# Attention rows: both images of a step taken together, and the middle channel tile ahead of the third

## What is computed

```
x = x + outlook(group_norm(x))    # 6 heads, softmax over 3x3 neighbours, weighted values, projection
x = x + window(group_norm(x))     # shifted 7x7 windows, 12 heads of 16 channels:
    qkv  = xw @ qkv_weight.T + qkv_bias
    attn = softmax(q * hd**-0.5 @ k.T + rel_pos_bias + mask)
    out  = (attn @ v) @ proj_weight.T + proj_bias
```

## Time and profile before

| what | value |
|---|---|
| median of three runs | 3687.9 us |
| the profiled execution | 3694.54 us, of which its span is 3692.7 us |
| mean granted TensorE clock | 0.949 of full speed |
| PE busy | 3321.1 us, 90% of the span |
| DVE, POOL, ACT busy | 74%, 65%, 51% |

### The profile page before, as it was taken

The page is one execution under the profiler, slowest core; times in us unless marked ns, Lnnn a source line. Parts: engine busy times, 40 slices in busy tenths (PEclk is TensorE's granted clock), DMA queues, the critical chain, the costliest instruction groups (busy, mean ns, idle before and its releaser), DMA issues.

```text
span 3692.7 us, 105251 instructions
## 1 busy us (share of the span) xinstructions
PE 3321.1 (90%) x39908; PEld 1964.0 (53%) x39908; DVE 2743.5 (74%) x4465; ACT 1869.8 (51%) x3602; POOL 2413.9 (65%) x1888
## 2 busy tenths in 40 slices
PE   5999989899899988988889888898989989899988
PEld 3456644566445664456643566346663466634665
DVE  4967779677796777967779677786767867687676
ACT  3445544555435554455543555435554455544555
POOL 2767747676476764767647676477765777566774
PEclk7999989999899998999989999999989999899998
DMA  4732237222371223712246222561215512165122
GB/s 105 141 80 67 73 77 138 65 82 62 84 142 49 83 75 76 143 52 75 76 87 131 64 71 67 105 128 56 83 50 115 121 52 84 55 126 110 56 74 60
DMA packets 204343, 317.51 MB, mean 86 GB/s; under 512 B 16922, under 2 KB 176154, under 8 KB 203802
## 3 DMA queue, kind: packets, MB, share of 16 engines
q0 software_dynamic: 31936, 148.66, 20.7%
q1 hardware_dynamic: 171866, 161.61, 15.0%
HBM read 45.97 MB, written 38.54 MB: 23 GB/s over the span
## 4 chain that ended last, share of the span: by engine, by line
PE 44%; POOL 16%; issue 16%; ACT 11%; DVE 8%; DMA 4%; DVEq 0%; POOLq 0%; SPq 0%; ACTq 0%
POOL sp__70 L1767 6%; POOL sp__70 L1774 4%; PE P L485 4%; DMA prod<-prod 4%; PE P L726 3%; PE P L649 3%; PE P L713 3%; DVE prod L1419 3%; POOL xr L1760 3%; PE P L647 3%; PE P L651 3%; ACT kbd L1095 2%; ACT kbd L1094 2%; DVE sp__70 L1523 2%; PE P L694 2%
## 5 line engine op out<-in xcount | busy, mean ns | idle before, releaser
L1774 POOL TENSOR_TENSOR sp__70<-sp__70,rc 128x588 f32<-128x588 f32 x512 | 600.9, 1174 | 465.1 <-DVE rc L1540 459.2
L1419 DVE TENSOR_TENSOR prod<-P,vpad 128x896 f32<-128x896 f32 (+1 forms) x768 | 791.3, 1051 | 140.1 <-PE P L485 126.7
L1537 DVE TENSOR_REDUCE sm<-sp__70 128x12 f32<-128x588 f32 x512 | 390.8, 763 | 479.7 <-ACT sp__70 L1112 479.6
L1767 POOL TENSOR_TENSOR sp__70<-sp__70,mx 128x588 f32<-128x588 f32 x512 | 598.0, 1173 | 217.8 <-DVE mx L1530 217.6
L1112 ACT ACTIVATE sp__70<-sp__70 128x588 f32<-128x588 f32 x512 | 358.2, 700 | 706.0 <-POOL sp__70 L1767 705.9
L485 PE MATMUL P<-at,sel 108*128 108x448 bf16 x1512 | 429.5, 363 | 63.1 <-DVE prod L1419 32.9
L1523 DVE TENSOR_TENSOR sp__70<-P,relb 128x588 f32<-128x588 f32 x512 | 389.6, 761 | 119.8 <-PE P L713 114.1
L1687 POOL DMA_DIRECT2D prod<-prod x216 | 202.5, 941 | 373.4 <-DVE prod L1419 369.9
L1530 DVE TENSOR_REDUCE mx<-sp__70 128x12 f32<-128x588 f32 x512 | 389.3, 760 | 9.1
L1120 ACT ACTIVATE pt<-P 98x588 f32<-98x588 f32 x512 | 311.7, 663 | 128.6 <-PE P L726 126.7
L726 PE MATMUL P<-ident,sp__70 113*98 113x113 f32 x3072 | 354.2, 267 | 19.5 <-DVE sp__70 L1523 19.5
(11 more groups left out here) (255 smaller groups left out, 7356.9 us busy)
## 6 DMA issues: line engine op xcount, KB each, us to landing
prod<-prod POOLq DMA_DIRECT2D x216, 672.0 KB, 5.6
vbd<-vs SPq DMA_DIRECT2D x512, 147.0 KB
xin<-in_x SPq DMA_DIRECT2D x126, 336.0 KB, 4.2
out<-ot SPq DMA_DIRECT2D x184, 168.0 KB, 3.6
out<-ot SPq DMA_DIRECT2D x80, 84.0 KB
wn<-in_L_conv_qkv_weight SPq DMA_DIRECT2D x2, 432.0 KB, 6.1
wno<-in_L_conv_proj_weight SPq DMA_DIRECT2D x2, 144.0 KB, 6.6
self<-in_sel SPq DMA_DIRECT2D x3, 91.1 KB
```

Source lines behind the costliest of these rows:

```text
L1419: tt(by_row(dst), by_row(P[:, b:b + len(op), 0:CT]), val, ALU.mult).then_inc(prod_ok, 1)
L1537: red(sm[:, b, :], sp_[:, b, :].rearrange("p (h k) -> p h k", h=NH), AX.X, ALU.add).then_inc(p_sum, 1)
L1767: tt(per_head(sp_[:, b, :]), per_head(sp_[:, b, :]), spread(mx[:, b, :]), ALU.subtract).then_inc(t_sub, 1)
L1774: tt(per_head(sp_[:, b, :]), per_head(sp_[:, b, :]), spread(rc[:, b, :]), ALU.mult).then_inc(p_norm, 1)
```

## The change

It has five parts.

1. **The tile order in rows.** Queries, keys, the projection, and their keeping and finishing come as tile 0, tile 1, tile 2 (`ROW_ORDER`) in banks R0, R2, R1 (`ROW_BANKS`). In `end`, the middle tile's matmul stands ahead of the third tile's. `begin` writes the middle tile's bank first, so it may start before the third one's bank is free: the wait for that one (`freed`) stands inside it.
2. **The Y bank's wait** moves from ahead of `scores` to ahead of `attend` (`y_bank_free`). The transposes of the next pair's input move: tiles 0, 1, 2 from steps 1, 2, 2 to steps 2, 2, 3. Where `window_values(w + 1, 0)` waited for two finished tiles of the row before, it now waits for three.
3. **ACT** takes probabilities of image 0, exponential of image 0, probabilities of image 1, exponential of image 1. Before, the exponential of image 0 stood at the end of the step ahead.
4. **DVE** does the finishing and the statistics at the start of a step, both sums after them; the third `finish` of a row stays at the start of step 3.
5. **POOL** shifts both images, stages, normalizes both images. The residual's addition `xa + bout` becomes `xa * one + bout`, with a column of ones.

```diff
+ROW_ORDER, ROW_BANKS = (0, 1, 2), (R0, R2, R1)
@@ PE
-                def begin(banks, bank, w, col, src, n):
+                def begin(banks, bank, w, col, src, n, freed=None):
...
+                    if freed is not None:
+                        pe.wait_ge(*freed)
                     mm(a, w[LO, 1, col:col + 128], src[LO, 1], start=True, stop=False)
...
                     elif p == 0:
+                        end_queries(w + 1)
                         if w >= 2:
                             pe.wait_ge(y_kept, ONE + PAIRS * R)
                             turn_out(w - 2, 1, Y_BANK)
-                        end_queries(w + 1)
-                        if w >= 2:
                             pe.wait_ge(q_kept, ONE + T * (R + 1) + 1)
                             turn_out(w - 2, 2, R0)
-                            pe.wait_ge(ot_kept, ONE + NT * (R - 2) + 2)
...
                     elif p == 2:
+                        end_out(w - 1)
                         pe.wait_ge(y_kept, ONE + PAIRS * R + 2)
-                        turn_next(w, 1, Y_BANK)
-                        end_out(w - 1)
+                        turn_next(w, 0, Y_BANK)
                         pe.wait_ge(fin_ok, ONE + T * (R - 1) + 1)
-                        turn_next(w, 2, R0)
-                        pe.wait_ge(x_kept, x_count + 2)
+                        turn_next(w, 1, R0)
...
+                def y_bank_free(w, p):
+
+                    R = NW * i + w
+                    x_count = ONE + T * (CHUNKS * (i + 1) + w - 1)
+                    if w >= 2 and p < 2:
+                        pe.wait_ge(ot_kept, ONE + NT * (R - 2) + 2 * (p + 1))
+                    elif w >= 1 and p >= 2:
+                        pe.wait_ge(x_kept, x_count + (1 if p == 2 else 3))
...
                     elif p == 1:
-                        pe.wait_ge(k_kept, ONE + T * (R + 2))
-                        pe.wait_ge(x_kept, x_count + 1)
-                        begin_out(w - 1)
+                        pe.wait_ge(k_kept, ONE + T * (R + 1) + 2)
+                        begin_out(w - 1, freed=(k_kept, ONE + T * (R + 2)))
                     elif p == 2:
-                        pe.wait_ge(fin_ok, ONE + T * (R - 1) + 2)
-                        pe.wait_ge(x_kept, x_count + 3)
+                        pe.wait_ge(fin_ok, ONE + T * (R - 1) + 3)
+                        pe.wait_ge(x_kept, x_count + 2)
                         window_values(w + 1, 0)
@@ ACT, window_row
                         keep_probs(w, p, 0)
+                        w1, p1 = pair_after(w, p, 1)
+                        exp_step(w1, p1, 0)
                         keep_probs(w, p, 1)
-                        w1, p1 = pair_after(w, p, 1)
                         exp_step(w1, p1, 1)
                         late(w, p)
-                        w2, p2 = pair_after(w, p, 2)
-                        exp_step(w2, p2, 0)
@@ DVE, window_row
-                        if w >= 1 and p == 3:
-                            finish(w - 1, 2, R2)
+                        if w >= 1 and p == 2:
+                            finish(w - 1, 0, ROW_BANKS[0])
+                            finish(w - 1, 1, ROW_BANKS[1])
+                        elif w >= 1 and p == 3:
+                            finish(w - 1, 2, ROW_BANKS[2])
...
                         prob_sum(w1, p1, 0)
-                        if w >= 1 and p == 2:
-                            finish(w - 1, 0, R0)
                         prob_sum(w1, p1, 1)
...
                         ahead(w, p)
@@ POOL
-                    pool.tensor_scalar(by_window(xr[:, w % 2, j, :]), rows(w, j), bout[:, j:j + 1], None,
-                                       ALU.add).then_inc(xr_ok, 1)
+                    pool.tensor_scalar(by_window(xr[:, w % 2, j, :]), rows(w, j), one[:], bout[:, j:j + 1],
+                                       ALU.mult, ALU.add).then_inc(xr_ok, 1)
...
+                        if w == NW - 1 and p == 0:
+                            stage_residual(w, 2)
                         if w1 < NW:
+                            shift_step(w1, p1, 0)
                             shift_step(w1, p1, 1)
-                            normalize_step(w1, p1, 0)
```

More of the change, by code:

```diff
@@ L122, in mixer @@
         fence = sb("fence", [128, 1])
+        one = sb("one", [128, 1])
         mv = sb("mv", [128, T, 2])
@@ L655, in end @@
                     b = P[:, banks[1], 0:n]
-                    second = mm(b, w[:, 2, col + 64:col + 192], src[:, 2], start=False, stop=True)
-                    return second, mm(P[:, bank, 0:n], mid[:, k, :], src[:, 1], start=False, stop=True)
+                    second = mm(P[:, bank, 0:n], mid[:, k, :], src[:, 1], start=False, stop=True)
+                    return second, mm(b, w[:, 2, col + 64:col + 192], src[:, 2], start=False, stop=True)
                 def begin_queries(w, lo=0, bank=R2):
@@ L665, in end_queries, with begin_keys @@
                     third.then_inc(q_mm, 1)
-                def begin_keys(w, lo=0):
-                    begin((R0, R1), R2, wt, C, xw[:, w % 2, :, lo:RT], RT - lo).then_inc(k_mm, 1)
+                def begin_keys(w, lo=0, freed=None):
+                    begin((R0, R1), R2, wt, C, xw[:, w % 2, :, lo:RT], RT - lo, freed).then_inc(k_mm, 1)
                 def end_keys(w, lo=0):
@@ L673, in end_keys, with begin_out @@
                     third.then_inc(k_mm, 1)
-                def begin_out(w, banks=(R0, R1), bank=R2):
+                def begin_out(w, banks=(R0, R1), bank=R2, freed=None):
                     pe.wait_ge(y_kept, ONE + PAIRS * (NW * i + w + 1))
-                    begin(banks, bank, wot, 0, yt[:, w % 2, :, :], RT).then_inc(out_mm, 1)
+                    begin(banks, bank, wot, 0, yt[:, w % 2, :, :], RT, freed).then_inc(out_mm, 1)
                 def end_out(w, banks=(R0, R1), bank=R2):
@@ L900, in window_row @@
                             scores(w2, p2)
+                        if w < NW - 1:
+                            y_bank_free(w, p)
                         attend(w, p)
@@ L1250, in _ @@
                 keep_keys(0, 0, R0, EDGE)
-                keep_keys(0, 1, R1, EDGE)
                 exp_step(0, 0, 1)
-                keep_keys(0, 2, R2, EDGE)
-                for n, bank in enumerate((R0, R1, Y_BANK)):
+                keep_keys(0, 1, R2, EDGE)
+                keep_keys(0, 2, R1, EDGE)
+                for n, bank in enumerate((R0, Y_BANK, R1)):
                     keep_queries(0, n, bank, EDGE)
-                exp_step(0, 1, 0)
                 for m in range(2):
@@ L1591, in last_row @@
                     w, Gn = NW - 1, CHUNKS * (i + 1)
+                    stat_x(i + 1, w - 2, range(T))
                     prob_sum(w, 1, 0)
                     prob_sum(w, 1, 1)
-                    stat_x(i + 1, w - 2, (1, 2))
                     ahead(w, 0)
@@ L1608, in last_row @@
                     coefficients(2 * i + 2)
-                    finish(w - 1, 1, R1)
-                    finish(w - 1, 2, R2)
+                    finish(w - 1, 1, ROW_BANKS[1])
+                    finish(w - 1, 2, ROW_BANKS[2])
                     prob_sum(w, 3, 0)
@@ L1622, in last_row @@
                     finish(w, 0, R1)
-                    finish(w, 1, R2)
-                    finish(w, 2, Y_BANK)
+                    finish(w, 1, Y_BANK)
+                    finish(w, 2, R2)
                 score_bias(0, 0, 0)
@@ L1653, in _ @@
             pool.memset(self32[:], 0.0).then_inc(zeroed, 1)
+            pool.memset(one[:], 1.0)
             pool.memset(eps_s[:], EPS).then_inc(zeroed, 1)
+            pool.wait_ge(zeroed, 4)
             def bias_tiles(dst, v):
```

83 lines of the change are left out of this document (39 added, 44 removed).

## The result

The changed kernel takes 3874.03 us, the median of four runs (3863.96 to 3883.53), and the kernel before 3691.23 on the same chip (four runs, 3683.56 to 3704.27). The ratio is 1.049, with a 95% interval of 1.045 to 1.054. It is slower, as forecast, but by 183 us and not by 102, and the time lies outside the range. One run of the last experiment was slow (11482.34 us at a granted clock of 0.581) and is left out of its median.

A forecast was written before the change was run, and what follows sets the result against it. PE's order list and the freeing of banks bound a row (PE busy 29.85 of 32.73 us). 3694.5 + 126 for 48 rows - 24 for the last rows = 3797 for a profiled execution, so 3790; range 3728 to 3850.

The forecast's parts named there:

- Step 1: Second step of an attention row: two waits and a moved turn go, small new waits come; 9.29 to 8.0 us.
- Step 2, the stall: Third step of a row: PE waits 3.45 us for DVE's third finish ahead of `window_values`; 7.16 to 10.6 us.
- rival D: No stall, since the third tile is finished as early as the first two; row 30.8 us, total 3531, chance 0.06.
- Step 0: First step of a row: the 0.70 us wait of the scores for ACT's output copy vanishes; 8.00 to 7.3 us.
- The clock: Half clock behind each row's stall: 4 us of PE work at half clock, costing 2.0 us a row.
- The base: Average row of the kernel before, half clock included, from which the growth was counted: 33.57 us.
- Row 7: Last row of each iteration: PE's 2.68 us wait ahead of the first scores shrinks; 3 us an iteration, -24 in all.
- Row 0 and the outlook stage stay: First row of each iteration and the outlook stage: claimed unchanged, with no term in the sum.
- `xr` at nothing: POOL's residual addition in two-operand form: may rid POOL of 115 us, none on PE's path, so no gain counted.

The follow-up runs named there:

- the last experiment: ACT's alternation of probability copies and exponentials taken out of rows 1 to 6 of the fastest version (finish, spreads, start and row 0 repaired): 3564.33 us against 3562.23.
- The two repairs: On the changed kernel with early third finish and spreads first (3596.89 us): key copies and their wait reordered at iteration start, 3577.14; then row 0's probability copies before exponentials, 3562.23.

## Why the prediction was wrong, point by point

The direction, the place and the mechanism of the largest term were right; a row grew by 3.40 us where its sum gave 2.6, and the edges of each iteration were left out of the sum.

- **Step 1: right.** 8.01 against 8.0. The new waits are the ones named: 0.20 for the probability copy, 0.15 and 0.25 for the keys; one more of 0.25 for an output copy.
- **Step 2, the stall: right, a little too long.** 3.10 us in each of 48 rows against 3.45; the 0.3 that I added for DVE's later list wasn't there. The experiment with the third finish early shows it as the cause, and that rival D named the right condition (when the third finish is ready). Without the stall a row takes 31.74 us (D had 30.8), and the time is 3632.
- **Step 0: the step that failed.** I wrote that the wait of 0.70 vanishes, and left 7.3 us for the step, with no term for the value spread. It vanished, but `attend` waits for the value spread, 39.8 us in all, and the step takes 7.9 to 8.8 in rows 2 to 6. The moved `turn_next` was counted as four transposes on PE. Its semaphore was not followed into SP's queue, where a load waits for it and the spreads stand behind the load. Moving the spreads ahead gave back 44 us. That wait is +0.83 a row; with -0.35 for the stall it makes 0.48, and the row without half clock is 34.69 against the predicted 34.2.
- **The clock: right.** Of the 4.98 us a row at half clock 4.43 lie on work, and they are worth 2.05, against 4 and 2.0. Some of it does fall into the stall, as I wrote: 0.55 us a row, in 28 of the 48 stalls. The Trainium skill's page "TensorE: Matmul & The Clock Gate", section "HAM oscillation — how this bites in real kernels", prices such a stall at half of the throttled time. By that rule a row would lose 2.42 for 4.84 us, and the runs show 2.05; with the 0.55 in the stall left out the rule gives 2.15.
- **The base.** I took 33.57 for a row before, read between marks on POOL; between PE's own turns it is 33.34. With the two points above that is the whole gap in a row: 0.48 + 0.05 + 0.23 = 0.76, times 48 = 36 us.
- **Row 7: half right.** PE's wait ahead of the scores fell from 2.68 to 0.27 us, and step 0 by 4.4 us on average, but step 1 grew by 2.3. There, in seven of eight iterations, PE now waits some 1.15 us for DVE's first finish ahead of the next group norm's means (`L360`), and the half clock in it rose from 1.8 to 4.4 us on average. By an estimate the two make up the 2.3: 1.0 us more of idle time, and 1.3 for 2.6 us more of half clock. In all the last rows came to -19 us against the forecast -24. From PE's timeline of the changed kernel, in the first iteration:

```profile
493.76 0.88 PE L718 MATMUL P<-kbd,qs 32*64 32x98 f32 x48 [0.27 <-ACT xa L964]
...
502.71 1.49 PE L360 MATMUL P<-mv,gm 128*128 128x1 f32 x12 [1.15 <-DVE fin L1563]
```

- **"Row 0 and the outlook stage stay": wrong.** +11 and +18 us. The diff changes the start of each iteration and row 0's order on ACT, and I gave them no sum. The two repairs take back 35 us.
- **`xr` at nothing: right in its number, wrong in its reason.** "PE waited for none of its work" looked one releaser deep. In the old order this part alone is worth 57 us; in the new order it is worth nothing.

The gap is 36 in the rows, 5 in row 7, 11 in row 0 and 18 from there on, 70 of the 71 us between the forecast for a profiled execution (3797) and 3868.24. The other 13 of the 84 us are the distances of the two profiled executions from their medians. The range was too narrow because it took in only bounds of terms that I had named.

What stays open: how the remaining gain of the new order over the kernel with the new `xr` form alone (30.94 against 32.40 us a row) is shared among the bank order, the Y bank's wait and DVE's and POOL's orders. These were not run apart. The start of an iteration kept 1.7 us of its loss (189.18 against 187.51). A wait of 1.49 us against 1.16 and the half clock in three of eight iterations are part of it; the rest isn't shown.

## What to carry to other kernels

When an instruction is moved, follow every semaphore that it increments into every queue, DMA issue queues above all, and read what stands behind the waiting entry there; a free-looking move of four small matmuls cost 44 us so. When a wait names an engine that is little used, ask what that engine itself was waiting for, until a busy one is reached: the 0.70 us put down to ACT was POOL's. And give every piece of the program that the diff touches a term, the first and last rows too.

## What the runs showed of the hardware

- Around stalls of 3.1 us the granted clock fell anywhere from 1.6 us before the work resumed to 1.6 us after (47 of 48 stalls), and stayed low for 3.4 or 6.8 us. Of 4.98 us at half clock in a row 0.55 lay in the stall, so most of the stall's clock cost lies in the work after it.
- Spare matmuls in the wait kept the clock at 1.00 and made the kernel 92 us faster, though they do no work of it.
- GpSimd adds a column to a 128x392 float32 tile in 1284 ns in the one-operand form and in 688 ns as multiply and add with two columns.
